# Attention: the products of queries and shifted keys are made on GpSimd, between its updates, instead of on VectorE

## The reference, cut to what matters

```python
C = jnp.einsum('bhtd,bhsd->bhts', w, w) * beta[:, :, None, :]
L = jnp.where(tri_s, C, 0.0) + jnp.eye(T, dtype=x.dtype)
Rhs = jnp.where(tri_s, jnp.einsum('bhtd,bhjd->bhtj', w, k), 0.0)
A = jax.scipy.linalg.solve_triangular(L, Rhs, lower=True, unit_diagonal=True)
qw = jnp.where(tri, jnp.einsum('bhid,bhtd->bhit', q, w), 0.0)
S = jnp.einsum('bhid,bhjd->bhij', q, k) - jnp.einsum('bhit,bhtj->bhij', qw, beta[..., None] * A)
logits = S * scale + (G[..., :, None] - G[..., None, :])
P = jax.nn.softmax(logits, axis=-1)
o = jnp.einsum('bhij,bhjd->bhid', P, v)
```

## Time and profile before

| | |
|---|---|
| time, median of 3 runs | 2345.96 us (2341.86 to 2352.36) |
| the profiled execution | 2352.26 us, span 2350.1 us |
| mean granted TensorE clock | 0.903 of full speed |
| PE busy | 2055.5 us, 87% of the span |
| DVE busy | 1644.5 us, 70% |
| ACT busy | 869.7 us, 37% |
| POOL busy | 836.0 us, 36% |
| POOL's updates of the recurrence | 83.7 us (L456, 120 instructions) and 180.9 us (L462, 240) |

### The profile page before, as it was taken

One profiled execution on the slowest core, in us unless ns is written; L12 is line 12 of the kernel. 1 busy time (PEld: TensorE's weight loads), 2 busy tenths in 40 slices (PEclk: granted clock), 3 DMA queues, 4 the chain that ended last, 5 costly groups with the idle time before them and its releaser, 6 DMA issues. The chain is left out here.

```text
span 2350.1 us, 44343 instructions
## 1 busy us (share of the span) xinstructions
PE 2055.5 (87%) x16519; PEld 1373.3 (58%) x16519; DVE 1644.5 (70%) x3673; ACT 869.7 (37%) x1694; POOL 836.0 (36%) x871
## 2 busy tenths in 40 slices
PE   4798998988988898898898899989799999788885
PEld 2573564564555465456456456766799998345443
DVE  5968759839938947856874883540366765999996
ACT  2022233223224234133222322312166653887782
POOL 1523413622532532451352254130366653222211
PEclk7898999989989989889898888987899999899997
DMA  3000000000000000000000000120622223100000
GB/s 108 10 3 15 1 2 15 11 12 15 4 19 15 1 20 17 1 20 3 14 13 10 15 4 18 37 97 1 238 72 72 72 71 90 49 18 28 5 9 14
DMA packets 70189, 72.63 MB, mean 31 GB/s; under 512 B 12976, under 2 KB 58592, under 8 KB 69840
## 3 DMA queue, kind: packets, MB, share of 16 engines
q1 hardware_dynamic: 61296, 51.75, 7.4%
q0 software_dynamic: 8672, 17.91, 2.2%
HBM read 38.05 MB, written 27.43 MB: 28 GB/s over the span
## 5 line engine op out<-in xcount | busy, mean ns | idle before, releaser
L664 ACT ACTIVATE a_prep<-ps 128x1536 f32<-128x1536 f32 (+1 forms) x112 | 155.6, 1389 | 349.8 <-PE ps L1310 207.3
L905 DVE TENSOR_REDUCE a_mpart<-ps 128x4 f32<-128x512 f32 x320 | 199.6, 683 | 56.8 <-PE ps L1251 33.7
L1853 ACT ACTIVATE b_hid<-ps,b_stage 128x128 f32<-128x128 f32 x572 | 162.8, 368 | 143.9 <-PE ps L1968 132.0
L1838 POOL DMA_INDIRECT rows_y<-b_orow,b_target x143 | 164.7, 1152 | 123.9 <-DVE b_orow L1943 120.6
L462 POOL TENSOR_TENSOR a_X<-a_X,a_txy 128x480 f32<-128x480 f32 (+14 forms) x240 | 180.9, 771 | 64.5 <-DVE a_txy L855 63.3
L456 POOL TENSOR_TENSOR a_K<-a_K,a_yU 128x480 f32<-128x480 f32 (+14 forms) x120 | 83.7, 697 | 331.0 <-DVE a_yU L850 329.8
L1129 PE MATMUL ps<-a_txy,cst 128*128 128x480 f32 (+14 forms) x480 | 181.7, 485 | 11.0 <-DVE a_txy L837 10.3
L1977 PE MATMUL ps<-b_stage,b_hid 128*128 128x128 f32 x1144 | 151.4, 276 | 1.5 <-ACT b_hid L1853 1.5
L1968 PE MATMUL ps<-b_hTp,b_stage 128*128 128x128 f32 x1144 | 151.2, 275 | 0.0
L207 PE MATMUL ps<-cst 128*128 128x128 f32 x862 | 133.7, 303 | 15.8 <-issue 10.3
L872 DVE TENSOR_TENSOR a_mats<-ps,cst 128x512 f32<-128x512 f32 x112 | 69.9, 684 | 100.9 <-PE ps L1158 100.9
(11 more groups left out here) (467 smaller groups left out, 4578.5 us busy)
## 6 DMA issues: line engine op xcount, KB each, us to landing
b_hrow<-rows_h SPq DMA_DIRECT2D x143, 65.0 KB
b_w<-in_wexp SPq DMA_DIRECT2D x16, 514.0 KB
d_got<-rows_y SPq DMA_DIRECT2D x32, 256.0 KB, 4.0
rows_h<-a_txy SPq DMA_DIRECT2D x19, 325.0 KB
rows_y<-b_orow,b_target POOLq DMA_INDIRECT x143
out<-xs SPq DMA_DIRECT2D x8, 256.0 KB, 2.3
cst<-in_const SPq DMA_DIRECT2D x1, 1865.5 KB, 15.0
rows_h<-a_mats,r_slot POOLq DMA_INDIRECT x112
```

Of the source, the lines that this page charges most:

```text
L664: nc.scalar.activation(Pt[:, at:at + width, :], ps[:, 4:4 + width, :], ACT.Exp).then_inc(e_exp.sem, width)
L905: nc.vector.tensor_reduce(mpart[:, i, j, 4 * g:4 * g + 4], ps[:, 4 + n % 4, :].rearrange("p (r j) -> p r j", r=4), AX.X, ALU.max).then_inc ...
L1838: nc.gpsimd.indirect_dma_start(yrows, bass.IndirectOffsetOnAxis(target[:, p % DEEP:p % DEEP + 1], 0), orow[:, p % DEEP, :], None).then_inc ...
L1853: last = nc.scalar.activation(hid[:, p % 2, f, :], ps[:, p % 2, 128 * f:128 * f + 128], ACT.Gelu, bias=stage[:, p % 3, AT_B1 + f:AT_B1 + f ...
```

## The change

`products` moves word for word from DVE to POOL. There `products(d - 1)` stands at the head of step d, behind the two updates X of step d - 1 and ahead of update U of step d. It gains a wait for update U of its own step and for the clearing of `tS8`. The strings of the orders lose 15 letters f on DVE and gain 15 on POOL in each stage. Arithmetic, buffers and PE's order are as before.

```diff
@@ -446,9 +446,24 @@ (POOL, front)
+                def products(d):
+                    n = NC * (C - d)
+                    yield
+                    po.wait_ge(*e_uU(d - 1))
+                    if d >= 2:
+                        po.wait_ge(*e_pS(d - 2))
+                    if d == 8:
+                        po.wait_ge(*setup_pool(1))
+                    dst = chunks(tS8[:, :])[:, :, d:C] if d == 8 else tS[:, d % 2, 0:n].rearrange("p (c s) -> p c s", c=NC)
+                    nc.gpsimd.tensor_tensor(dst, chunks(qf[:, :])[:, :, d:C], chunks(K0[:, :])[:, :, 0:C - d],
+                                            ALU.mult).then_inc(e_tS.sem, 1)
+
                 for d in range(1, C):
                     n = NC * (C - d)
                     left, right = slice(0, C - d), slice(d, C)
+                    if d >= 2:
+                        yield from products(d - 1)
                     yield
                     po.wait_ge(*e_yU(d - 1))
                     po.wait_ge(*e_tS(d - 1))
@@ -461,6 +476,8 @@
                                                 ALU.subtract).then_inc(e_uX.sem, 1)
+                yield from products(C - 1)
@@ -809,15 +826,6 @@ (DVE, front)
-                def products(d):
-                    n = NC * (C - d)
-                    yield
-                    if d >= 2:
-                        ve.wait_ge(*e_pS(d - 2))
-                    dst = chunks(tS8[:, :])[:, :, d:C] if d == 8 else by_chunk(tS[:, d % 2, 0:n])
-                    nc.vector.tensor_tensor(dst, chunks(qf[:, :])[:, :, d:C], chunks(K0[:, :])[:, :, 0:C - d],
-                                            ALU.mult).then_inc(e_tS.sem, 1)
@@ -836,8 +844,6 @@
-                    if d >= 2:
-                        yield from products(d - 1)
@@ -854,9 +860,6 @@
-                yield
-                ve.wait_ge(*e_uU())
-                yield from products(C - 1)
```

More of the change, by code:

```diff
@@ L135 @@
            'bbbbfffbbbbfbfbbfbbbbbbbfffbbbbbbbfffbbbbbbbfffbbbbbbbfbbbbbbbfbbbbbbbbbfbbbbbbbfbfbb'),
-    've': ('fbbfbfbbbbfffffffbbfbffffbfbfffffffffffbbbbffffbbbbffffbbbbffffbbbbffbbbbffbbbbffbbbbffbbbbffbbbbffb'
-           'bbbfbfbfbbbfbfbffffffbbfbbbbbbbbfbbbbbbffbfbfbbbbffbfffbffffffffffffffffffbfffbfffffffffffbfffffffff'
-           'ffffffffffffbffffffffffffffbbbbbbfffbbbfffbb'),
+    've': ('fbbfbfbbbbfffffffbbfbffffbfbfffffffffffbbbbffffbbbbfffbbbbffffbbbbfbbbbffbbbbffbbbbffbbbbfbbbbffbbbb'
+           'fbfbfbbbbfbfffffbbfbbbbbbbbfbbbbbbffbfbfbbbbfbfffbfffffffffffffffbfffbfffffffffbffffffffffffffffffbf'
+           'ffffffffffffbbbbbbfffbbbfffbb'),
     'act': ('bbffbbfbbfffbfbfffffbbbffbfffbfbbbbbbbbbbbbbbbbbbbbbbbfbfbbbb'),
-    'po': ('bbbbbbbfffffffffffffffbfffbfbbbfbbfbbfffffffffffffffffffffffffff'),
+    'po': ('bbbbbbbfffffffffffffffffffbffffbfbbbfbbffbbffffffffffffffffffffffffffffffffffff'),
 }
@@ L149 @@
            'bbbbbfffbbbbfbfbbfbbbbbbbfffbbbbbbbfffbbbbbbbfffbbbbbbbfbbbbbbbfbbbbbbbbbfbbbbbbbfbfbb'),
-    've': ('fbbfbfbbbbfffffffbbfbffffbfbfffffffffffbbbbffffbbbbffffbbbbffffbbbbfrfrbbbbffbrbbbffbbbbffbbbbffbbbb'
-           'ffbbbbfbfbfbbbfbfbffffffbbfbbbbbbbbfbbbbbbffbfbfbbbbffbfffbffffffffffffffffffbfffbfffffffffffbffffff'
-           'fffffffffffffffbffffffffffffffbbbbbbfffbbbfffbb'),
+    've': ('fbbfbfbbbbfffffffbbfbffffbfbfffffffffffbbbbffffbbbbfffbbbbffffbbbbfrrbbbbffbrbbbffbbbbffbbbbfbbbbffb'
+           'bbbfbfbfbbbbfbfffffbbfbbbbbbbbfbbbbbbffbfbfbbbbfbfffbfffffffffffffffbfffbfffffffffbfffffffffffffffff'
+           'fbfffffffffffffbbbbbbfffbbbfffbb'),
     'act': ('bbffbbfbbfffbfbfffffbbbffbfffbfbbbbbbbbbbbbbbbbbbbbbbbfbfbbbb'),
-    'po': ('bbbbbbbfffffffffffffffbfffbfbbbfbbfbbfffffffffffffffffffffffffff'),
+    'po': ('bbbbbbbfffffffffffffffffffbffffbfbbbfbbffbbffffffffffffffffffffffffffffffffffff'),
 }
@@ L160 @@
     'act': ('brrbffbbfbbfffbfbfffffbbbffbfffbfbbbbbbbbbbrrrrbbbbrbrbbbbbbbbfbfbbbb'),
[L161 to L164, removed]
+    've': ('frbrbfbfbbbbfffffffbbfbffffbfbfffffffffffbbbbffffbbbbfffbbbbfffrfbbbbfbbbbffbbbbffbbbbffbbbbfbbbbffb'
+           'bbbfbfbfbbbbfbfffrffbbfbbbbbbbbfbbbbbbffbfbfbbbbfrbfffbrffrffrfrfrrfrfrrfffffrrfrfrrrrrrrbfrffbffrfr'
+           'ffffffbffffffffffffffffffbfffffffffffffbbbbbbfffbbbfffbb'),
+    'po': ('bbbbbbbfffffffffffffffffffbffffbfbbbfbbffbbffffffffffffffffrfrfffrfrfffrfrfffrfrfffrrffffrrrrrr'),
 }
```

## The result

The changed kernel takes 2373.04 us (median of 4 runs, 2367.89 to 2377.08), the one before in the same runs 2344.55. The ratio is 1.0115, with a 95% interval of 1.0083 to 1.0146: slower by about 27 us, where 12.8 were forecast, and above the range.

The account below looks back on a forecast made before the run. No engine was taken as full; DVE and POOL taking turns on SBUF and the recurrence's circle decide. Terms 4.5 - 1.2 + 5.7 + 2.8 - 1.4 + 2.4 = +12.8 us on the median 2345.96 gave 2359 us; range 2347 to 2370.

Parts of the forecast that it names:

- steps 10 to 15: Late steps of stages 1 to 7: POOL's products stand ahead of its DMA issues, where it has waiting time; 0.
- stages that change by more than 3 us: Sign against the forecast: stages 1 to 7 changing by more than 3 us each with the granted clock.
- Stage 0: Stage 0's recurrence: slower products on POOL take turns with DVE's tX and stay on the circle; +4.5 us.
- Step 2 in the loop: Loop stages: the product holds up the L1620 behind the second update X, so L905 come 0.95 later; +5.7 us in all.
- Step 5: Stages 1 to 7: the product runs among the two tX, 0.87 less 0.47 saved on DVE; +2.8 us in all.
- Steps 1, 3, 4: Stages 1 to 7: products hide under L905; only product 1 in stages 5 to 7 saves time; -1.2 us in all.
- step 7: Stages 1 to 7: the product hides under a long reduction and 0.2 of DVE's saving remains; -1.4 us in all.
- steps 8 and 9: Small routing instructions and tX are delayed, +0.35 and +0.25; counts in stages 1 to 4, where DVE is dense; +2.4 us.
- Stages absorb it: Rival: idle times in the loop take up the delays; only stage 0 and L1620 stay, +4 to +10 us; chance 0.26.
- +8.3 forecast: Stages 1 to 7: the prediction's terms for these stages together, +8.3 us.
- Faster: Rival: DVE is the limit and POOL's product is free; 6.3 us less in stage 0, 24 in all; chance 0.08.
- Clock: Rival: the shift changes stages' length through TensorE's clock, 12 us more or 12 less; chance 0.08 each way.

Follow-up runs that it names:

- e6: The kernel before, all products left on DVE, with one piece fewer in DVE's front stream: ratio 1.0136, +31 us.
- e1: The kernel before with products moved to GpSimd (POOL) in stage 0 only: ratio 1.0023 (0.9997 to 1.0048).
- e5: The changed kernel with one empty piece added to DVE's front stream, restoring the order of before: ratio 1.0063 (1.0027 to 1.0099).
- e10: The changed kernel run again as it is, on the chip of the split: ratio 1.0164 (1.0115 to 1.0212), median 2374.82 us.
- e11: The changed kernel with one empty piece added to DVE's front stream, on the chip of the split: ratio 1.0018 (0.9983 to 1.0053), median 2349.92 us.
- e12: The kernel before with all products on GpSimd in stages 1 to 7 and on VectorE in stage 0: ratio 1.0009 (0.9976 to 1.0041).
- e9: The kernel before, unchanged, run for its trace on the chip of the split: 2326.59 us in its one run.
- e4: The kernel before with one VectorE memset of 2048 columns put ahead of stage 0: ratio 1.0036 (1.0019 to 1.0054).
- e7: The kernel before with one empty piece added in DVE's front stream behind the last product: ratio 1.0183 (1.0123 to 1.0244).

## Why the prediction was wrong

- **The step that failed** is the count of what moves, not a price. The sum has a term for each product and each instruction beside it, and ends with the recurrence: steps 10 to 15, "0". What stands behind the recurrence on DVE has no term. The section on the change says that the strings lose 15 letters f, and of the place it shows that everything else stands as it stood. Neither was set against the number of pieces taken out, 16. DVE's written order has nine blocks in place of eight ahead of the copy in each of stages 1 to 7; it was there to be read. Measured alone, in e6, this is +31 us, more than double the whole forecast. One of the forecast's own signs of being wrong, stages that change by more than 3 us, came in six of the seven stages; but it was tied to the granted clock, and the mean clock of stage 2 was nearly that of before (0.89 and 0.90).
- **Stage 0, +4.5:** the mechanism was right. The recurrence grew by 3.0 us in the change, and was 59.5 or 59.6 in e1, e5, e10 and e11 too, against 56.3 to 56.6 with the products on DVE. In step 5 the pair of tX grew by 0.80, and 0.47 was saved, so 0.33 instead of 0.5: the first tX took less of the turn from POOL's product than assumed. The term was 1.5 too large.
- **Step 2 in the loop, 0.95 a stage:** seen, even as +1.28 in e12 (four L1620 in 2.56 us where the earlier trace rows has 1.86, and 0.6 more at the round of maxima behind them). It did not reach the end of the stage.
- **Step 5, 0.4 a stage:** in e12 the delay against e9 grew from 0.77 us ahead of the yU of step 5 to 1.47 at that of step 7, so 0.7. It was taken up as well.
- **Steps 1, 3, 4, -1.2; step 7, -1.4; steps 8 and 9, +2.4:** too small to be told apart. The reason given for the last one, that DVE is dense up to the raw output copy, does not hold in e9, where it idles 1.04 us ahead of it.
- **Stages absorb it** (chance 0.26) is the right case for the products in stages 1 to 7: +8.3 forecast, +2 measured by e12 (-6 to +10), and 187.7 us against 187.7 in undisturbed stages. For the products alone the whole would be stage 0's 3.0 and little more. The ratios of e5 and e11 don't decide: by e5 it is 6 to 23 us, by e11 -4 to +12, by their mean 9.
- **Faster** (0.08): refuted by the tX that are held up, and by e1, whose interval ends at -0.7 us where 6.3 less was claimed for stage 0. **Clock:** no case of its own in the change, but its part is real: 1.2 us of the 4.8 at the end of stage 2 are matmuls at the lower clock behind PE's idle time. Stages of equal code differ by 3 to 4 us, as the rival said: stages 2 and 5 in the earlier trace rows. The clock goes with it, but no run varies it alone. One stage in e12 and one in e11 take 197.7 us at a clock of 0.86 and 0.85, 10 us more than their neighbours. Both kernels have the products on GpSimd there and the order of before; whether such stages are part of what the products cost was not looked into.

Whether the remaining cost of the products is 3, 9 or 12 us stays open; e4 shows that 8 us may come from a mere shift.

## What to carry to other kernels

Where streams are woven by strings of letters, taking work out of a stream is two edits, the pieces and the letters, and they must agree in number and in place; a string one letter too long or too short moves everything behind it, with no error. So read the difference of the orders to its last row, count pieces against letters, and ask of every row that moved what it now waits for and what stands behind it. Here the row was far from the edit and cost some 25 to 34 us, while the edit itself, argued through step by step, cost some 3 to 12; a delay of half a microsecond inside a stage is worth nothing until it is followed to the wait that ends the stage.

## What the runs showed of the hardware

- DVE's and POOL's instructions on SBUF take turns, one instruction each, and both engines' get longer: tX 1.75 to 2.55 us a pair, and POOL's product 12.96 us over the 15 of stage 0 where the same sizes took 10.47 in the earlier trace rows. The Trainium skill, "SBUF — State Buffer", section "Who interferes with whom", calls the pair of ports that the two engines share an exclusive lock, for which the order of issue decides who waits; the trace agrees, with a tX that ends only behind POOL's product, the pair 0.80 us longer.
- Waits of PE can cost again afterwards: behind idle times of 1.37 and 2.42 us in stage 2 of the change the granted clock fell from 1.00 to 0.50, and matmul groups took 1.12 and 2.07 us instead of 0.66 and 1.16. It came with every end of a stage that has nine blocks ahead of the copy (0.76 to 0.88 from the copy on) and with none that has eight (0.97 to 1.00).
- The profiled execution of e7 took 4643.76 us, the other six 2341 to 2363. Its granted clock reads 1.000 throughout, and yet its matmuls are about twice as long, while DVE is busy for 134.24 us in its stage 2, as in the others. This group of e7

```profile
L1969 PE MATMUL ps<-b_hTp,b_stage 128*128 128x128 f32 x1144 | 374.7, 537 | 0.0
```

has a mean of 537 ns, and the change, in its own page, 275:

```profile
L1971 PE MATMUL ps<-b_hTp,b_stage 128*128 128x128 f32 x1144 | 151.1, 275 | 0.0
```

The granted clock did not show it; only the lengths did. It is one execution, and its cause is not known.
